# Moving TensorE's early transposes into one run, lookups into seven pieces, and more table rows to ScalarE, in a DLRM tower kernel

## What is computed

```python
e = jnp.stack([tbl_0[ids[:, 0]], ..., tbl_31[ids[:, 31]]], axis=1)   # [2048, 32, 256]
z = einsum('bnd,bmd->bnm', e, e)[:, iu, ju]                          # 496 pairs i < j
h = jnp.concatenate([z, dense_ctx], axis=1)                          # [2048, 512]
h = jnp.maximum(h @ W_top1 + b_top1, 0.0)                            # 512
h = jnp.maximum(h @ W_top2 + b_top2, 0.0)                            # 256
y = h @ W_top3                                                       # 1
```

## Time and profile before

| what | us |
|---|---|
| median of 3 runs | 548.25 (546.71 to 550.8) |
| the profiled execution's own time | 548.03 |
| its span, first to last instruction | 546.2 |
| TensorE matmuls busy | 503.2 (92%) |
| GpSimd busy | 390.7 (72%) |
| VectorE busy | 250.8 (46%) |
| ScalarE busy | 184.0 (34%) |

### The profile page before, as it was taken

The page is one execution under the profiler, slowest core; times in us unless marked ns, Lnnn a source line. Parts: engine busy times, 40 slices in busy tenths (PEclk is TensorE's granted clock), DMA queues, the critical chain, the costliest instruction groups (busy, mean ns, idle before and its releaser), DMA issues.

```text
span 546.2 us, 27461 instructions
## 1 busy us (share of the span) xinstructions
PE 503.2 (92%) x11015; PEld 464.7 (85%) x11015; DVE 250.8 (46%) x592; ACT 184.0 (34%) x355; POOL 390.7 (72%) x418
## 2 busy tenths in 40 slices
PE   0765899999899999999999999999999999999997
PEld 0764799999789899998998989898899988888996
DVE  3665563543536244363625436362543536244142
ACT  1777151421505133050514215050521505142152
POOL 6777767777777777777777777777777777777710
PEclk9998999999999999999999999999999999999999
DMA  8999634444444444444444444454444444443310
GB/s 194 253 254 282 196 101 117 132 119 122 127 122 130 122 122 119 129 116 121 130 123 121 131 123 119 118 131 120 119 131 122 121 124 122 117 115 108 109 32 2
DMA packets 39173, 71.19 MB, mean 130 GB/s; under 512 B 11302, under 2 KB 25382, under 8 KB 39046
## 3 DMA queue, kind: packets, MB, share of 16 engines
q0 software_dynamic: 19728, 53.90, 35.2%
q1 hardware_dynamic: 18550, 15.14, 11.4%
q10 hardware_dynamic: 768, 0.39, 0.3%
HBM read 69.39 MB, written 0.01 MB: 127 GB/s over the span
## 4 chain that ended last, share of the span: by engine, by line
PE 60%; POOL 18%; issue 9%; DMA 7%; DVE 3%; ACT 1%; SPq 1%; DVEq 0%
PE look_ps L395 22%; POOL rows L347 18%; PE quad_ps L417 13%; PE top_ps L476 7%; PE quad_ps L379 6%; PE turn_ps L379 6%; DMA landed<-in_tbl 4%; PE top_ps L497 4%; DMA rows<-in_tbl,row_ids 2%; PE quad_ps L438 1%; DMA ids_across<-in_small_ids 1%; DVE turned L725 1%; PE top_ps L461 1%; DVE one_hot L797 1%; DVE small L787 1%
## 5 line engine op out<-in xcount | busy, mean ns | idle before, releaser
L347 POOL DMA_INDIRECT rows<-in_tbl,row_ids x411 | 390.0, 949 | 129.1 <-issue 114.1
L395 PE MATMUL look_ps<-one_hot,small 125*128 125x256 f32 (+1 forms) x1536 | 220.8, 293 | 8.6 <-DVE small L787 8.5
L395 PEld LDWEIGHTS look_ps<-one_hot,small 125*128 125x128 f32 x1536 | 195.0, 193 | 12.4 <-issue 9.9
L797 DVE TENSOR_SCALAR one_hot<-ids_across,sub_row 125x256 fp32r<-125x256 int32 (+1 forms) x384 | 118.2, 378 | 121.4 <-PE look_ps L395 112.4
L417 PE MATMUL quad_ps<-turned 128*32 128x31 f32 x7680 | 105.0, 199 | 3.5 <-issue 2.2
L417 PEld LDWEIGHTS quad_ps<-turned 128*32 128x32 f32 x7680 | 86.6, 110 | 23.8 <-issue 5.0
L570 ACT ACTIVATE ahead<-look_ps 128x512 f32<-128x512 f32 (+1 forms) x48 | 28.0, 584 | 203.5 <-PE look_ps L395 203.4
L379 PE MATMUL turn_ps<-ident,rows 128*128 128x128 f32 x418 | 62.9, 281 | 20.2 <-DMA rows<-in_tbl,row_ids 16.3
L379 PEld LDWEIGHTS turn_ps<-ident,rows 128*128 128x128 f32 x418 | 46.7, 142 | 24.8 <-issue 17.8
L379 PE MATMUL quad_ps<-ident,rows 128*128 128x128 f32 x404 | 61.1, 280 | 6.5 <-DMA rows<-in_tbl,row_ids 4.3
L561 ACT ACTIVATE turned<-turn_ps 128x512 f32<-128x512 f32 x57 | 36.1, 633 | 60.7 <-PE quad_ps L417 44.8
(11 more groups left out here) (68 smaller groups left out, 199.3 us busy)
## 6 DMA issues: line engine op xcount, KB each, us to landing
area<-in_tbl SPq DMA_DIRECT2D x640, 1.0 KB
rows<-in_tbl,row_ids POOLq DMA_INDIRECT x411
area<-in_tbl ACTq DMA_DIRECT2D x384, 1.0 KB
ids_across<-in_small_ids SPq DMA_DIRECT2D x45, 128.0 KB
landed<-in_tbl SPq DMA_DIRECT2D x6, 896.0 KB
w_sb<-in_W_top SPq DMA_DIRECT2D x4, 256.0 KB
landed<-in_tbl SPq DMA_DIRECT2D x6, 104.0 KB
w_sb<-in_W_top SPq DMA_DIRECT2D x1, 512.0 KB
```

The lines of the kernel that those rows point to most:

```text
L347: pool.indirect_dma_start(out=rows[:, n % PLACES, j, :], out_offset=None, in_=tables[f], in_offset=bass.IndirectOffsetOnAxis(ap=row_ids[:, ...
L395: last = pe.matmul(look_ps[:, c * width:(c + 1) * width], small[:, f, r, part, c * P:(c + 1) * P], one_hot[n % 2][:, r, 0:width], start=(r ...
L797: last = dve.tensor_scalar(one_hot[n % 2][:, r, 0:width], ids_across[0:SP, n % IDS_RING, 0:width], sub_row[:, r:r + 1], None, ALU.is_equal)
```

## The change

- The four early turnings of tile t+1 stand in one run behind portion 6 of tile t, for t > 0.
- The lookups are cut in seven pieces, ahead of portions 1 to 6 and behind portion 7: the first field in three pieces of 10 or 11 matmuls, the other two in two pieces of 16. No piece stands ahead of portions 0 and 7.
- In tile 0, portions 0 to 3 come first without any lookup; the fifth lookup stands whole ahead of portion 4, and the sixth in four pieces ahead of portions 5 to 7 and behind 7. The early turnings of tile 0 stay.
- ScalarE fetches rows for tiles 5, 8, 11 and 14 instead of 5, 10 and 14, each over the three tiles before, in chunks of 16, 16 and 12 rows (8 in the last). There is one indirect DMA less, 410 instead of 411. ScalarE's list of row numbers has another layout.
- SyncE loads the ids of the sixth lookup ahead of ScalarE's list, the dense features and the weights instead of after them.

```diff
-ACT_ROW_TILES = [5, 10, 14]
+ACT_ROW_TILES = [5, 8, 11, 14]
...
-    ACT_ROW_STAGES = 4
-    ACT_ROWS = [12, 12, 8]
+    ACT_ROW_STAGES = 3
+    ACT_ROWS = [[16, 16, 12], [16, 16, 12], [16, 16, 8]]
+    ACT_ROWS_AHEAD = [0, 44, 88]
...
-    EARLY_AFTER = [3, 4, 5, 6]
+    EARLY = 4
+    LOOK_AHEAD_OF = [1, 2, 3, 4, 5, 6, 8]
+    EARLY_AFTER = 6
...
+            load_ids(5)
             sp.dma_start(act_list_sb[:, :], act_list).then_inc(act_list_in, 16)
...
-            load_ids(5)
             for t in range(TILES):
...
+            def first_look(k):
+                fifth, sixth = FIRST[0], FIRST[0] + 1
+                if k == PARTS // 2:
+                    look_up(fifth, 0, PRODUCTS)
+                if k > PARTS // 2:
+                    at = k - PARTS // 2 - 1
+                    look_up(sixth, PRODUCTS * at // (PARTS // 2), PRODUCTS * (at + 1) // (PARTS // 2))
...
                 made = FIRST[t + 1] - FIRST[t]
+                if k not in LOOK_AHEAD_OF:
+                    return
+                piece, pieces = LOOK_AHEAD_OF.index(k), len(LOOK_AHEAD_OF)
                 for n in range(made):
-                    begin, end = (n * (PARTS + 1) + made - 1) // made, ((n + 1) * (PARTS + 1) + made - 1) // made
-                    if begin <= k < end:
-                        look_up(FIRST[t] + n, PRODUCTS * (k - begin) // (end - begin),
-                                PRODUCTS * (k + 1 - begin) // (end - begin))
+                    begin, end = (n * pieces + made - 1) // made, ((n + 1) * pieces + made - 1) // made
+                    if begin <= piece < end:
+                        look_up(FIRST[t] + n, PRODUCTS * (piece - begin) // (end - begin),
+                                PRODUCTS * (piece + 1 - begin) // (end - begin))
...
                 for k in range(PARTS):
-                    look_between(t, k)
+                    if t > 0:
+                        look_between(t, k)
+                    else:
+                        first_look(k)
...
                     if 0 < t < TILES - 1 and k == 0:
                         layer2(t - 1)
-                    early_after = EARLY_AFTER if t > 0 else FIRST_EARLY_AFTER
-                    if k in early_after and t + 1 < TILES:
-                        turn(BEGIN[t + 1] + early_after.index(k))
-                look_between(t, PARTS)
+                    if t == 0 and k in FIRST_EARLY_AFTER:
+                        turn(BEGIN[1] + FIRST_EARLY_AFTER.index(k))
+                    if t > 0 and k == EARLY_AFTER and t + 1 < TILES:
+                        for i in range(EARLY):
+                            turn(BEGIN[t + 1] + i)
+                if t > 0:
+                    look_between(t, PARTS)
+                else:
+                    first_look(PARTS)
```

More of the change, by code:

```diff
@@ L24 @@
 TILES = BATCH // P
+ACT_LISTED = 44
+ACT_LIST_AT = [0, 44, 84]
 ACT_ROW_FIELD = FIELDS - 3
-ACT_ROW_TILES = [5, 10, 14]
+ACT_ROW_TILES = [5, 8, 11, 14]
 def pair_order():
@@ L72, in dlrm_tower @@
     ACT_ROW_UNIT = len(PAIRED) - 2
-    ACT_ROW_STAGES = 4
-    ACT_ROWS = [12, 12, 8]
+    ACT_ROW_STAGES = 3
+    ACT_ROWS = [[16, 16, 12], [16, 16, 12], [16, 16, 8]]
+    ACT_ROWS_AHEAD = [0, 44, 88]
+    LISTED = ACT_LISTED
     ROW_FIELD = FIELDS - 1
@@ L158, in dlrm_tower @@
         ident = sbuf("ident", [P, P])
-        act_list_sb = sbuf("act_list_sb", [ACT_ROW_STAGES * len(ACT_ROW_TILES), P // ACT_ROW_STAGES], int32)
+        act_list_sb = sbuf("act_list_sb", [ACT_ROW_STAGES * len(ACT_ROW_TILES), LISTED], int32)
         y_sb = sbuf("y_sb", [P, TILES])
@@ L501, in turn_all @@
             def turn_all(t):
-                for i in range(len(EARLY_AFTER), BEGIN[t + 1] - BEGIN[t]):
+                for i in range(EARLY, BEGIN[t + 1] - BEGIN[t]):
                     turn(BEGIN[t] + i)
@@ L643, in fetch_rows @@
                     return
-                stage, at = t - ACT_ROW_TILES[i] + ACT_ROW_STAGES, sum(ACT_ROWS[:chunk])
+                stage = t - ACT_ROW_TILES[i] + ACT_ROW_STAGES
+                many, at = ACT_ROWS[stage][chunk], ACT_ROWS_AHEAD[stage] + sum(ACT_ROWS[stage][:chunk])
                 if stage == 0 and chunk == 0:
@@ L651, in fetch_rows @@
                 _, numbers = nc.values_load_multi_w_load_instructions(
-                    act_list_sb[listed:listed + 1, at:at + ACT_ROWS[chunk]], engines=[mybir.EngineType.Activation],
+                    act_list_sb[listed:listed + 1, at - ACT_LIST_AT[stage]:at - ACT_LIST_AT[stage] + many], engines=[mybir.EngineType.Activation],
                     min_val=0, max_val=tables[ACT_ROW_FIELD].shape[0] - 1,
@@ L655, in fetch_rows @@
                 for k, number in enumerate(numbers):
-                    p = stage * P // ACT_ROW_STAGES + at + k
+                    p = at + k
                     act.dma_start(act_row_field[p:p + 1, :], tables[ACT_ROW_FIELD][bass.ds(number, 1), :],
@@ L699, in _ @@
                 kept = range(FIRST[t], FIRST[t + 1] - 1)
-                for chunk in range(len(ACT_ROWS)):
+                for chunk in range(len(ACT_ROWS[0])):
                     fetch_rows(t, chunk)
@@ L850 @@
     laid["row_list"] = np.ascontiguousarray(by_slot[:, FIELDS - 1].reshape(1, BATCH))
-    laid["act_list"] = np.ascontiguousarray(by_slot[:, ACT_ROW_FIELD].reshape(TILES, P)[ACT_ROW_TILES].reshape(-1, P // 4))
+    laid["act_list"] = np.ascontiguousarray(
+        np.stack([by_slot[t * P + at:t * P + at + ACT_LISTED, ACT_ROW_FIELD] for t in ACT_ROW_TILES for at in ACT_LIST_AT]))
     laid["ids"] = np.ascontiguousarray(by_slot.reshape(TILES, P, FIELDS).transpose(1, 0, 2))
```

## The result

The changed kernel takes 627.19 us (median of four; the kernel before, 547.6 in the same runs). The ratio of the two is 1.141, with a 95% interval of 1.133 to 1.150; it leaves out the slowest run, 634.09 us, which the median counts. The change makes the kernel slower, as forecast, and by more: 600 us was said, with 577 to 620. The profiled execution took 622.4 us with a span of 620.6. The four early turnings in one run do what the prediction says, the chunks of 16 too. Of the 22.6 us by which the span is longer than forecast, about 12 are TensorE's clock; the rest is several smaller terms.

A forecast was written before the change was run, and what follows sets the result against it. GpSimd was taken as the bound before; after, a loop of TensorE and GpSimd through the nine-place ring. T(1) 73.8, T(2) 108.9 and twelve loops give T(14) 541.7, span 598.0, so 600 us; range 577 to 620.

The forecast's parts named there:

- What bounds the kernel: Before the change: GpSimd, issuing indirect DMAs at a step of 1.25 us without rest, is the bound, TensorE a hair behind.
- Early turnings in one run: Unit 0's turning starts at T + 22.2 instead of T + 14.2 (T: layer 1's start); GpSimd waits at unit 9.
- The wait of layer 2: With no lookup between portion 0 and layer 2, TensorE stands 0.7 us until the relus end.
- ScalarE's chunk: Chunks of 16 rows delay the second field's copy, so the third lookup waits 1.75 us in tiles 2 to 13.
- Tile 0: Portions and turnings fill TensorE's 6.29 us wait; tile 1's last DMA landing sets T(1) at 73.8, where it was 78.8.
- the loop: TensorE waits for unit 12, GpSimd for unit 0: 36.9 us per full tile, 35.65 with a helper.
- the wait goes: GpSimd's wait of 3.0 us at 74.74, for a place to be freed by TensorE, disappears with tile 0's order.
- The sum: T(1) 73.8, T(2) 108.9, twelve loops to T(14) 541.7, then the end: span 598.0, time 600 us.
- a rival with a chance of 0.13: TensorE's clock falls in each tile's new gaps, 14 x 1.2 to 1.5 us more: 617 to 621 us; chance 0.13.

The follow-up runs named there:

- experiment 11: The changed kernel with unread identity transposes added on TensorE: 13 ahead of unit 11, 4 ahead of unit 12, 10 ahead of the third lookup; 613.94 us, ratio 1.118.
- experiments 5 and 6: The changed kernel with the early turnings moved: all four behind portion 3 (560.94 us, ratio 1.025), or one behind each of portions 3 to 6 (560.61 us, 1.023).
- experiment 10: The changed kernel with 13 unread identity transposes ahead of units 11 and 12 and ahead of the third lookup; 623.14 us, ratio 1.136.

## Why the prediction was right or wrong

**What bounds the kernel.** Right. GpSimd at 72% busy was the bound: seven tiles with a helper and six full ones at its step of 1.25 us give 31.83 us on average, and T to T before is 31.84.

**Early turnings in one run.** Right in mechanism and place, and near in size. Forecast: unit 0 at T + 22.2 without a chunk and 23.95 with one, measured 22.3 in tile 1 and 23.6 to 24.8 in the tiles at a clock of 1.00; 0.87 us to unit 9, measured 0.93; one wait per tile at unit 9. Ten places for nine, and portion 3 for 6, took 45 and 66 us away with nothing else in TensorE's order changed.

**The wait of layer 2.** Right in kind, 0.2 to 0.5 us where 0.7 was said. By the prediction's own rows (4.9 less 4.3) it was 0.6.

**ScalarE's chunk.** Right: 1.57 us in tile 6 for 1.75, 1.0 to 2.0 in the twelve tiles, and about 20 us in the run without it for 21. What the prediction did not say is that it hangs on the seven pieces and on the place of the run; alone the chunks are a gain.

**Tile 0.** T(1) was 75.0 for 73.8. The wait was moved, not filled: TensorE stands 3.28 us for "issue" at 54.62, and T(1) then follows its own nine turnings, from 70.07 on, and not the landing that the prediction named. The gain there was swallowed by the loop, as said; taken alone it was smaller than the 3 us that the words "the wait goes" imply.

**The sum.** 598.0 us of span were forecast, 620.6 came, 22.6 more. By parts:

| where | us over the forecast |
|---|---|
| up to T(2): T(1) late, tile 1 | 1.6 |
| T to unit 0 in tiles 2 to 13, the part that goes in experiment 11 (the clock) | 11.7 |
| T to unit 0, the part that stays (mis-sized terms) | 2.8 |
| unit 0 to the next T, twelve loops | 7.6 |
| behind T(14) | -0.8 |

These make 22.9. From T to unit 0 it is 25.2 us on average for 23.95, and 24.2 in experiment 11. What stays there can be read in tile 6: the seven portions take 6.4 us for 5.7 and layer 1 3.67 for 3.49, against 0.35 less of waiting for the relus and 0.2 less for the copy. From unit 0 to the next T it is 152.6 us for 145.0, and hardly any of this is the clock. The prediction took 3.30 us from GpSimd's last DMA to layer 1; three full tiles have 3.3, but seven tiles with a helper have 3.7 to 4.0, which is 3.6 us in all. In tile 5 unit 12 landed late (4.29 us of waiting at 226.22), which is another 2.9. 0.93 for 0.87 us to unit 9 makes 0.7, and tile 4, where the clock fell, 0.4.

**The step that failed** is the treatment of the clock: "the new gaps are two or three of about 2 us with turnings between", and therefore a rival with a chance of 0.13 and nothing in the sum. The gaps were of that length, most of them 1.0 to 2.7 us and one of 4.3, and the clock fell at ten of the 25 places. A mean clock of 0.970 over 620 us is a loss of 18.6 us of full speed, in 37 us at half speed; before it was 0.994, 3.3 us. The rows of before showed one gap of 6.3 us behind which it fell and one of 1.9 behind which it did not. Between these I took the shorter for the rule, where the honest reading was that a gap of 2 to 4 us had no row. The price of a fall was right: 1.2 to 1.5 us were said, and 11.7 us for the nine falls that experiment 11 has less are 1.3 each. The number of falls was not: the rival had fourteen. So it is partly luck that its 617 to 621 us lie near the 622.4 of the profiled execution. With the clock alone the sum would have come to some 612 us, inside 577 to 620; the other terms of the table, some 11 us, brought the rest. Two further runs have lower clocks and longer times (622.4 us at a mean clock of 0.970, 627.0 at 0.967, 627.4 at 0.962); the lower clock can explain a part of that.

The page of the Trainium skill on TensorE's clock (TensorE: Matmul & The Clock Gate, HAM oscillation) has a loop in which a wait for a DMA takes the clock down anew in every turn. This trace agrees in part: the clock fell again and again, but only 6 of the 13 loops from tile 1 on have a mean of 0.96 or less, and it fell behind a wait for ScalarE's copy as well as behind landings. The waits of the page's loop, about 3 to 5 us, are longer than all but one of these, so the page did not make this case the likely one, as the prediction has it. The Trainium skill's page on reading traces (Perfetto Trace Analysis, Optimization Strategy) says that a gap repeating on the engine that should be saturated can mean too few buffers; here it appeared at unit 9 of every tile, and one buffer more took 45 us off.

**Open:** why the pair products wait more for "issue" in the kernels with seven pieces and chunks of 16, which is a part of the 2.3% of experiments 5 and 6; and why unit 12 of tile 5 landed late.

## What to carry to other kernels

Where a ring of buffers connects two engines that are both nearly full, write down the loop: from the first release in a turn, through the producer's remaining steps, to the consumer's next turn. As long as it is shorter than the slower engine's own period (27.1 us for 31.25 to 32.5 here) the order of releases is free; eight us later it was the bound, and no busy share said so beforehand. Collecting small pieces of work into one run is such a move of releases. And where rows show TensorE's clock falling behind a long gap and have none for the length that the change brings, put it into the sum with the share of gaps at which it may fall (here ten of 25, at some 1.3 us each), not as an unlikely case beside it.

## What the runs showed of the hardware that was not expected

- In the changed kernel the granted clock fell to 0.50 at gaps of 1.7 to 4.3 us (once at two gaps of 1.5 and 1.0 with a turning between), and not at others of up to 2.65 us. So the length of the gap does not settle it. Each fall lasted some 3 us.
- Transposes of the identity in the gaps, 13 in each, held it at 1.00 in all thirteen loops (experiment 10); with 13, 4 and 10 it was 1.00 in twelve of them, and 13 us were won by 27 more TensorE instructions a tile (733 for 706).
- ScalarE issues single-row DMAs at 0.37 us each, 5.99 us for 16, and has the first of 16 out 1.6 us behind the start of the copy ahead of them (279.12 to 280.76).
